# A gated linear attention stage on one core: root of the mean square moved to GpSimd, states joined, matmuls of neighbouring heads interleaved

## The reference, cut to what matters

```python
q1, k1, v = h @ Wq * 64**-0.5, h @ Wk, h @ Wv
q2 = (h @ Wqa @ Wqb) * 64**-0.5
k2 = softmax((h @ Wka @ Wkb).reshape(B, L, 8, 64), axis=-1)
gk1 = log_sigmoid(h @ Wg1a @ Wg1b + bg1) / 16
gk2 = log_sigmoid(h @ Wg2a @ Wg2b + bg2) / 16
e = softmax(h @ We); mask = one_hot(top1(e)); rw = e * mask
def chunk_gla(q, k, v, gk):                 # per head, chunks of C = 64 tokens
    g = cumsum(gk, within chunk); qg = q * exp(g); kg = k * exp(-g)
    A = tril(qg @ kg.T); o_intra = A @ v
    # S is carried from chunk to chunk
    o_inter = qg @ S; S = S * exp(g_last) + (k * exp(g_last - g)).T @ v
    return o_intra + o_inter
o = chunk_gla(q1, k1, v, gk1) + sum(chunk_gla(q2*rw[e], k2*rw[e], v, gk2*mask[e]) for e in range(4))
o = o * rsqrt(mean(o*o, -1) + 1e-5) * norm_w
g = h @ Wga @ Wgb
out = x + gate * ((o * g * sigmoid(g)) @ Wo)
```

## Time and profile before

| | us |
|---|---|
| median of 3 runs (5705.07 to 5719.47) | 5708.47 |
| the profiled execution | 5707.32 |
| its span from first to last instruction | 5705.6 |
| first instructions of the linear attention stage | 4591.8 |
| first and last Square of its 32 tiles (L2105) | 4665.4, 5691.2 |
| a tile without a stretch of low TensorE clock, and the next one | 32.3, 33.5 |

### The profile page before, as it was taken

One profiled execution on the slowest core, in us unless ns is written; L12 is line 12 of the kernel. 1 busy time (PEld: TensorE's weight loads), 2 busy tenths in 40 slices (PEclk: granted clock), 3 DMA queues, 4 the chain that ended last, 5 costly groups with the idle time before them and its releaser, 6 DMA issues. The chain is left out here.

```text
span 5705.6 us, 106962 instructions
## 1 busy us (share of the span) xinstructions
PE 4935.7 (87%) x37182; PEld 2590.9 (45%) x37184; DVE 4319.6 (76%) x5246; ACT 3134.2 (55%) x5403; POOL 940.8 (16%) x886
## 2 busy tenths in 40 slices
PE   6589999999999999999952548558999879999998
PEld 3233333333333333333332336435666556777776
DVE  4589999999999999999646313377665557777776
ACT  1068888888888888888841212112222234444443
POOL 0000000000000000000005740254320023334333
PEclk8689999999999999999965779879999979999998
DMA  5322333323322222222102027622110121000000
GB/s 184 110 93 89 103 101 99 96 91 100 101 90 78 80 82 82 76 83 80 46 33 75 16 65 226 198 91 70 59 37 1 65 69 27 24 22 22 27 23 14
DMA packets 241630, 431.82 MB, mean 76 GB/s; under 512 B 37946, under 2 KB 142411, under 8 KB 239009
## 3 DMA queue, kind: packets, MB, share of 16 engines
q1 hardware_dynamic: 197424, 355.18, 19.9%
q0 software_dynamic: 26928, 62.99, 3.4%
q10 hardware_dynamic: 16896, 8.39, 0.6%
HBM read 329.36 MB, written 133.89 MB: 81 GB/s over the span
## 5 line engine op out<-in xcount | busy, mean ns | idle before, releaser
L579 DVE TENSOR_REDUCE attn_mpart<-attn_ps_max 128x2 f32<-128x1024 f32 x2048 | 2498.5, 1225 | 114.2 <-PE attn_ps_max L617 105.8
L524 ACT ACTIVATE attn_probs<-attn_ps_exp 128x512 f32<-128x512 f32 x4096 | 2221.6, 595 | 344.7 <-PE attn_ps_exp L633 100.8
L617 PE MATMUL attn_ps_max<-attn_keys,attn_quer 54*128 54x512 f32 x4096 | 1502.0, 461 | 80.3 <-DMA attn_keys<-k_laid 53.2
L633 PE MATMUL attn_ps_exp<-attn_quer,attn_keys 54*128 54x512 f32 x4096 | 1501.9, 449 | 20.4 <-issue 13.4
L648 PE MATMUL attn_ps_out<-attn_probs,attn_vals 128*32 128x256 f32 x16384 | 1318.3, 394 | 8.4 <-ACT attn_o_sb L530 7.8
L633 PEld LDWEIGHTS attn_ps_exp<-attn_quer,attn_keys 54*128 54x128 f32 x4096 | 615.4, 186 | 874.5 <-ACT attn_probs L524 837.6
L648 PEld LDWEIGHTS attn_ps_out<-attn_probs,attn_vals 128*32 128x32 f32 x16384 | 323.9, 108 | 751.5 <-issue 396.4
L617 PEld LDWEIGHTS attn_ps_max<-attn_keys,attn_quer 54*128 54x128 f32 x4096 | 603.2, 190 | 121.6 <-DVE attn_mpart L579 63.5
L1371 POOL DMA_INDIRECT ra_rows<-y_rows,slots x256 | 255.0, 996 | 318.2 <-DVE ra_total L1538 246.5
L1442 PE MATMUL ra_psO<-ra_vals,ra_probT 128*128 128x256 f32 x1152 | 273.4, 383 | 7.1 <-DVE ra_probT L1616 7.0
L734 POOL DMA_INDIRECT x_rows<-pay,slots x256 | 256.5, 1002 | 126.6 <-issue 126.6
(11 more groups left out here) (324 smaller groups left out, 5997.5 us busy)
## 6 DMA issues: line engine op xcount, KB each, us to landing
attn_keys<-k_laid SPq DMA_DIRECT2D x256, 304.0 KB
attn_vals<-v_aug SPq DMA_DIRECT2D x128, 512.0 KB, 15.0
attn_keys<-k_laid SPq DMA_DIRECT2D x256, 128.0 KB
x_rows<-attn_zeros POOLq DMA_DIRECT2D x16, 1280.0 KB, 9.7
exp_x<-x_rows SPq DMA_DIRECT2D x64, 320.0 KB
exp_w1w<-in_w SPq DMA_DIRECT2D x64, 256.0 KB
y_rows<-exp_y SPq DMA_DIRECT2D x64, 256.0 KB
q_laid<-proj_parts SPq DMA_DIRECT2D x32, 256.0 KB
```

Source lines behind the costliest of these rows:

```text
L524: act.activation(probs[k % 2][:, j, :], ps_exp[bank_of(g, n)][:, :], ACT.Exp).then_inc(exp_done, 1)
L579: dve.tensor_reduce(mpart[i][:, kb, TC * pair + tile::TC * NPR], ps_max[u % 2][:, :, :], AX, ALU.max).then_inc(unit_read, 1)
L617: mm = pe.matmul(ps_max[u % 2][:, h, :], quer[g][half(h), pair, tile * P:(tile + 1) * P], keys[g % 2][half(h), pair, kb * CH:(kb + 1) * CH ...
L633: pe.matmul(ps_exp[bank_of(g, n)][:, :], keys[g % 2][half(h), pair, k * P:(k + 1) * P], quer[g][half(h), pair, :], start=True, stop=True). ...
```

## The change

Inside `linear_attention`:

1. `rms` leaves ScalarE. VectorE only reduces; the scale 1/64 moves into the Square; GpSimd adds the epsilon and raises to the power -0.5 (`root`), at the head of its iteration, before `queries`.
2. `norm_w` is multiplied into `wo` once at the start instead of into every tile's gate (L2265 goes); it is loaded with two small transfers in place of one.
3. The dense and the four sparse states become one array of five (`NS`), so that each pair of VectorE instructions on them becomes one.
4. `decay_sums` uses 64 columns of weights in place of 128, alternating between the two halves of the output rows, and comes between the dense and the sparse scores.
5. `scores` is split in two by kind and alternates even and odd heads; the sparse half waits for both dense masks. `keys_values` alternates the heads of a pair in its innermost loop; `intra` has two matmuls of 64 weight columns for each head.
6. VectorE scales and gates the output of `prv` between the dense and the sparse masks; ScalarE computes `decays` between Exp and Ln.

The core of the diff ("..." marks what is left out):

```diff
+        ms, power, eps = (sb(n, [P, HL]) for n in ("ms", "power", "eps"))
...
+                def root(tile):
+                    m, _, i = tile
+                    hold(pool, ms_ready, m + 1, pool_passed)
+                    pool.tensor_tensor(ms[:, :], ms[:, :], eps[:, :], ALU.add).then_inc(eps_added, 1)
+                    hold(pool, eps_added, m + 1, pool_passed)
+                    pool.tensor_tensor(ms[:, :], ms[:, :], power[:, :], ALU.pow).then_inc(rms_ready, 1)
...
                 def iteration(nxt, cur, prv):
+                    if prv is not None:
+                        root(prv)
                     queries(cur)
...
                     act.activation(lz[:, :, :], lz[:, :, :], ACT.Exp, scale=-1.0).then_inc(lz_step, 1)
+                    if cur is not None:
+                        decays(cur)
                     act.wait_ge(lz_step, 3 * m + 2)
                     act.activation(lz[:, :, :], lz[:, :, :], ACT.Ln, bias=1.0).then_inc(lz_step, 1)
...
-                    act.activation(sq[:, :, :], psO[:, :, :], ACT.Square).then_inc(squared, 1)
-
-                def rms(tile):
-                    m, _, i = tile
-                    act.wait_ge(ms_ready, m + 1)
-                    act.activation(ms[:, :], ms[:, :], ACT.Ln).then_inc(rms_step, 1)
-                    act.wait_ge(rms_step, m + 1)
-                    act.activation(ms[:, :], ms[:, :], ACT.Exp, scale=-0.5).then_inc(rms_ready, 1)
+                    act.activation(sq[:, :, :], psO[:, :, :], ACT.Square, scale=DK ** -0.5).then_inc(squared, 1)
...
+                dve.tensor_scalar(wo[:, :, :], wo[:, :, :], nw[:, 0:1], None, ALU.mult).then_inc(wo_set, 1)
...
-                    dve.tensor_reduce(ms[:, :], sq[:, :, :], AX, ALU.add).then_inc(o_step, 1)
-                    dve.wait_ge(o_step, m + 1)
-                    dve.tensor_scalar(ms[:, :], ms[:, :], 1.0 / DK, EPS1, ALU.mult, ALU.add).then_inc(ms_ready, 1)
+                    dve.tensor_reduce(ms[:, :], sq[:, :, :], AX, ALU.add).then_inc(ms_ready, 1)
...
-                        dve.tensor_tensor(s1_mid[part, :, x, :], s1_end[part],
-                                          dec1[part, :, 0].unsqueeze(2).to_broadcast([DK, NPAIR, DK]), ALU.mult)
-                        last = dve.tensor_tensor(s2_mid[part, :, :, x, :], s2_end[part],
-                                                 dec2[part, :, :, 0].unsqueeze(3).to_broadcast([DK, NPAIR, NE, DK]),
+                        last = dve.tensor_tensor(s_mid[part, :, :, x, :], s_end[part],
+                                                 dec[part, :, :, 0].unsqueeze(3).to_broadcast([DK, NPAIR, NS, DK]),
                                                  ALU.mult)
...
-                    mask_scores(cur)
+                    mask_scores(cur, 0)
                     if prv is not None:
+                        scale_o(prv)
                         gated(prv)
+                    mask_scores(cur, 1)
...
+                def scores(tile, kind):
+
+                    m, _, i = tile
+                    if kind:
+                        pe.wait_ge(scores_masked, 4 * m + 2)
+                    else:
+                        pe.wait_ge(feats_copied, 4 * m + 4)
+                    for b in range(NPAIR):
+                        for odd in range(2):
+                            r = odd * DK
+                            mm = pe.matmul(psW[1 - odd][:, b * P:(b + 1) * P], ftT[r:r + DK, 2 * kind, b, :],
+                                           ftT[r:r + DK, 2 * kind + 1, b, :], start=True, stop=True)
...
                     for b in range(NPAIR):
-                        pe.matmul(pdec1[:, b, :], ls[i][:, 0, b * P:(b + 1) * P], halves[:, :], start=True, stop=True)
+                        for odd in range(2):
+                            rows, head = slice(odd * DK, odd * DK + DK), slice((2 * b + odd) * DK, (2 * b + odd + 1) * DK)
+                            pe.matmul(pdec[rows, b, 0, :], ls[i][:, 0, head], halves[:, :], start=True, stop=True)
...
-                    for hh in range(HL):
-                        head, rows = slice(hh * DK, (hh + 1) * DK), slice(hh % 2 * DK, hh % 2 * DK + DK)
-                        for e in range(NE):
-                            pe.matmul(psS2[rows, hh // 2, e, :], ke[i][:, e, head], v[i][:, head], start=True, stop=True)
-                        mm = pe.matmul(kv1[rows, hh // 2, :], kg1[i][:, head], v[i][:, head], start=True, stop=True)
+                    for b in range(NPAIR):
+                        for e in range(NS):
+                            for odd in range(2):
+                                head, rows = slice((2 * b + odd) * DK, (2 * b + odd + 1) * DK), slice(odd * DK, odd * DK + DK)
+                                keys = ke[i][:, e - 1, head] if e else kg1[i][:, head]
+                                mm = pe.matmul(kv[rows, b, e, :], keys, v[i][:, head], start=True, stop=True)
...
-                        pe.matmul(psO[:, hh, :], a1[:, hh, :], v[i][:, hh * DK:(hh + 1) * DK],
-                                  start=(hh == 0), stop=False, skip_group_check=True)
+                        for late in range(2):
+                            rows = slice(late * GC, late * GC + GC)
+                            pe.matmul(psO[rows, hh, :], a1[:, hh, rows], v[i][:, hh * DK:(hh + 1) * DK],
+                                      start=(hh == 0), stop=False, skip_group_check=True)
...
                     ahead(ZG, K2)
+                    scores(cur, 0)
                     decay_sums(cur)
-                    scores(cur)
+                    scores(cur, 1)
                     ahead(Q2, V)
```

More of the change, by code:

```diff
@@ L1692 @@
 NPAIR = HL // 2
+NS = 1 + NE
 QSCALE = DK ** -0.5
@@ L2044, in iteration @@
                         keys(nxt)
-                run(pool, prologue, iteration, lambda tile: None)
+                run(pool, prologue, iteration, root)
             @block.scalar
@@ L2116, in iteration @@
                     if nxt is not None:
[L2117 to L2120 removed]
+                        log_sigmoids(nxt, cur)
+                    else:
+                        decays(cur)
                     if nxt is not None:
@@ L2157, in add_bias, with scale_o @@
                         dve.tensor_tensor(zb[:, x, :], psP[:, x, :], bias[:, x, :], ALU.add).then_inc(biased, 1)
-                def gated(tile):
+                def scale_o(tile):
                     m, _, i = tile
@@ L2165, in gated @@
                                       ALU.mult).then_inc(o_read, 1)
+                def gated(tile):
+                    m, _, i = tile
                     dve.wait_ge(o_read, m + 1)
@@ L2177, in center, with mask_scores @@
                                       ALU.subtract).then_inc(k_centered, 1)
-                def mask_scores(tile):
+                def mask_scores(tile, kind):
                     m, _, i = tile
-                    for x in range(4):
+                    for x in (2 * kind, 2 * kind + 1):
                         dve.wait_ge(scores_summed, 4 * m + x + 1)
@@ L2295, in epilogue @@
                     mean_square(tile)
+                    scale_o(tile)
                     gated(tile)
@@ L2419, in inter @@
                         o = psO[:, 2 * b:2 * b + 2, :].rearrange("p h d -> p (h d)")
-                        pe.matmul(o, ftT[:, 1, b, :], s1_mid[:, b, :, :].rearrange("p h d -> p (h d)"), start=False,
-                                  stop=False, skip_group_check=True)
-                        for e in range(NE):
-                            mm = pe.matmul(o, qeT[:, b, e, :], s2_mid[:, b, e, :, :].rearrange("p h d -> p (h d)"),
-                                           start=False, stop=(b == NPAIR - 1 and e == NE - 1), skip_group_check=True)
+                        for e in range(NS):
+                            queries = qeT[:, b, e - 1, :] if e else ftT[:, 1, b, :]
+                            mm = pe.matmul(o, queries, s_mid[:, b, e, :, :].rearrange("p h d -> p (h d)"),
+                                           start=False, stop=(b == NPAIR - 1 and e == NE), skip_group_check=True)
                     mm.then_inc(intra_inter, 1)
```

91 lines of the change are left out of this document (35 added, 56 removed).

## The result

The changed kernel takes 5555.1 us (median of 4 runs, 5544.37 to 5566.07) against 5711.43 for the kernel before (4 runs): a ratio of 0.9726, 95% interval 0.9702 to 0.9749. Forecast were 5613 us and a range of 5565 to 5670, so the gain was larger than even the range allows. The profiled execution took 5554.25 us, 153.1 less than the one before. The stage begins at the same time (4592.6 against 4591.8), so all of it lies inside.

What follows compares the result with a forecast made beforehand. TensorE looked like the bound, with a wait on ScalarE's root in its path. Tiles of 33.1 us become 30.15, saving 91 us over 31; with edges 95, 5707.3 to 5612, as median 5613 us, range 5565 to 5670.

Steps and rivals of the forecast that it cites:

- Clock again: TensorE's half-clock stretches in the last stage: 0.76 a tile as now, about 3.1 us each, adding 2.35 to 27.8 us.
- clean tile: Last-stage tile whose clock stays at full speed: predicted to go from 32.3 to 27.8 us.
- the edges: First tile gains about 3 us, last tile's root chain 1.8; one more SP-queue load costs 0.5.
- rival C: TensorE's clock holds because the low-work stretch is shorter: 73 us more saved, 5540 us; chance 0.15.
- K1 starts: TensorE's K1 projection, begun at +24.15 us into the tile before: predicted to start 4.85 us earlier.
- the 0.3 us added for VectorE's collisions: Allowance per clean tile for VectorE being close to the bound, up to 27 of 27.5 us busy; bounds 0 and about 1.
- the wait for dense masks: New TensorE wait of 1 us before the sparse scores, which need both dense masks.
- Keys and values: TensorE's 80 loads in keys_values: 3.55 us predicted to become 2.2, a gain of 1.35 us a tile.
- The claim that loads for different halves of the output rows overlap: TensorE weight loads alternating heads take 0.0275 us each, judged from four loads in 0.11 us of keys_values.
- the power: GpSimd's root: taken as 0.2 us like an add of 128 x 8, hidden, with 4.7 us left before scale_o.
- The collisions: VectorE held by GpSimd when both work from SBUF: 1.1 us for the gate, up to 2.2 for log_sigmoid.
- rival A: VectorE becomes the bound, late by 1 us more in every tile: 31 us lost, 5644 us; chance 0.15.

Runs made afterwards that it cites:

- decays_old: Changed kernel with decay sums 128 columns wide and ahead of all scores, as before: 5671.9 us, against 5715.2 for the kernel before on the same chip.
- before_decays: Kernel before with only the decay sums narrowed and put between dense and sparse scores: 5895.8 us, against 5893.0 for the kernel before on the same chip.
- root_scalar: Changed kernel with the root's Ln and Exp back on ScalarE and VectorE's gate after the masks: 5867.3 us, against 5906.5 for the kernel before.
- kv_by_head: Changed kernel with keys and values head by head again, not alternated: 5574.3 us, against 5715.2 for the kernel before on the same chip.
- pow_x4: Changed kernel with three more unused powers on GpSimd ahead of the one that counts: 5826.5 us, against 5907.0 for the kernel before.
- q2_in_wait: Changed kernel with Q2 moved ahead of the sparse scores, into the wait for the dense masks: 5739.5 us, ratio to the kernel before 0.972.
- add_after_ls: q2_in_wait with GpSimd's add of the scores held until VectorE's next log_sigmoid is done: 5716.9 us, against 5907.0 for the kernel before.
- combined: add_after_ls with G1 and G2 also ahead of the output projection: 5737.3 us, against 5907.0 for the kernel before on the same chip.
- decays_old_filled: decays_old with Q2 and V moved ahead of the sparse scores, into the mask wait: 5803.9 us, against 5906.5 for the kernel before.
- scores_grouped: Changed kernel with scores grouped by even and odd heads again, not alternated: 5567.9 us, against 5715.2 for the kernel before.
- two_products: combined without its hold and GpSimd's add; TensorE multiplies both score arrays by v and accumulates: 5513.42 us against 5716.36, ratio 0.9639.

## Why the prediction was wrong, point by point

*The step that failed* is the one headed **Clock again**: "With 0.76 of them a tile, as now". There were 7 stretches in 31 tiles and not 24, and four of them were the shorter ones of 3.4 us. It added 2.35 x 31 = 73 us to clean tiles; measured, the intervals lie 878.9 - 31 x 27.96 = 12 us above clean ones. That is 61 us. Of these, 56 are the clock: the first 30 intervals lie 17 us above clean ones. The other 5 are the last interval, 4.45 us shorter than a clean one, which the sum took for a full one. A clean tile 0.16 longer than predicted takes back 5, and the edges give 2: 153 saved, 95 predicted. This was rival C, at 0.15, with 5540 us.

I took the share of stretches for a property of the stage, though I had listed what TensorE did before they began: the very few-column and 64-row work whose run this change shortens from 5.2 to 4.1 us. The experiments show that the falls at this place hang on the run: undoing width and place of the decay sums brings them back (decays_old), with only one of the two undone the low time stays at 1.4 us, dense work put into the run takes it from 6.8 to 1.9, and a longer tile does not matter. They also show that the run is not all: with it cut but the root still on ScalarE (before_decays, root_scalar), falls come at the wait of some 3.2 us before the transposes. So it took both parts of the change to hold the clock. The argument against C, "there is a new 1 us wait beside it", counted the wait and did not add up the run: it gets shorter with the wait in it.

*Right:* the clean tile, 27.8 against 27.96, with a little luck: K1 starts 4.36 us earlier (19.79 us into the tile in place of 24.15) and not 4.85, and the 0.3 us added for VectorE's collisions covered most of that. The transposes stopped waiting; scores took 1.0 us (0.95 predicted), decay sums 1.0 (0.9), the wait for dense masks 0.82 (1.0), `intra` 1.15 behind a longer wait for `egn`. Keys and values took 2.5 us (2.2); the alternation gained 1.05 us of the 1.35. The claim that loads for different halves of the output rows overlap, which rested on four loads, is shown by 80: kv_by_head. The rule of the Trainium skill's page "TensorE: Matmul & The Clock Gate", section "The mechanism" of Part 3, that weight loads overlap only where the row group differs, would have given nothing there; this run speaks against it.

*Right for a reason partly wrong:* the power costs 1.65 us and not 0.2. It was hidden as predicted, with 2.4 us to spare (pow_x4).

*The collisions.* VectorE was expected to wait in the gate. In the clean tile shown the gate kept its 0.69 us and GpSimd's `qeT` stretched instead. Over the stage the gate took 1.35 on average, nearly as before (1.40). The price fell on `log_sigmoid`, 3.82 us beside GpSimd's add, or in other tiles on the decay of the states: 3.55 us for one of its two instructions, where the other takes 1.48. VectorE's 23.73 of 27.96 us busy still left room for it in the clean tile, so rival A did not come; q2_in_wait, add_after_ls and combined, at 28.2, are what it describes.

*Edges.* The first Square came 6.3 us earlier, 3 was predicted. The end gained nothing of its 1.8 us: the tail after the last Square is 14.5 us, 14.4 before. The chain of the last tile, before and then after:

```profile
5691.21 0.60 ACT gla_sq L2105
...
5691.83 1.28 ACT L2110
...
5694.88 0.70 DVE gla_on L2164
```

```profile
5538.03 0.61 ACT gla_sq L2114
...
5538.66 0.70 DVE gla_ms L2150
...
5539.88 1.68 POOLq L1947
...
5541.58 0.70 DVE gla_on L2163
```

From the start of the Square to `scale_o` it is 3.67 us before and 3.55 after. The old side of that term was right: two table loads and two short operations, with the reduction beside the first load. The new side was too small. It allowed for the reduction and two operations of 0.2 us; the power takes 1.68 us, and GpSimd's steps between the reduction, the add and the power another 0.3. The 1.8 us were used up by these.

*Left open:* why decays_old_filled and scores_grouped keep 2 us of low time, when the first has a shorter run than the kernel after, and how much each of the later waits adds. The runs show where TensorE had no dense work ahead of each fall, and no more than that.

## What to carry to other kernels

When the granted clock of a stage is below full speed, find what TensorE does ahead of each fall and ask first what the change does to it; a count of stretches must not be carried over as a constant. Cutting such a run with dense matmuls that are needed anyway brought the clock back here even where nothing got faster (decays_old_filled), as long as the time won did not turn into a wait further on (before_decays). And when instructions of VectorE and GpSimd that both work from SBUF collide, look first at which pairs meet: a hold on the wrong one changes nothing, as in add_after_ls. Giving the work to a third engine removed the collision here.

## What was unexpected of the hardware

- The clock also fell around waits of TensorE of 2.8 to 3.2 us: in the tiles shown, 0.6 us ahead of the wait's end in root_scalar, 1.2 us behind it in before_decays.
- A power of 128 x 8 values takes GpSimd 1.65 us, beside 0.20 for an add of the same size.
- A collision can fall on either engine. GpSimd's 128 x 8 multiply `half_masks`, 0.20 us, took 1.16 us on average in the kernel after, where it meets `log_sigmoid`; in two_products 0.25. Lines of the kernel after:

```profile
L2022 POOL TENSOR_TENSOR gla_a<-gla_a 128x1024 f32<-128x1024 f32 x30 | 94.3, 3145 | 0.6
...
L2016 POOL TENSOR_TENSOR gla_cme<-emask,gla_halves 128x8 f32<-128x8 f32 x30 | 34.9, 1163 | 0.0
```
